# The zero shifts of a query slot as a step of their own on SyncE, in a two-layer transformer block kernel

## What is computed

```python
def layer(x, c, context):
    x = x + gate_a * attention(modulate(ln(x)), modulate(ln(x)))   # layer 0: gate from c; layer 1: rotary q and k, no gate
    x = x + attention(ln(x), context)                              # layer 0: ln(context); layer 1: rotary, modulated
    return x + gate_m * mlp(modulate(ln(x)))                       # layer 0: tanh gelu, gate; layer 1: erf gelu, no gate

def attention(q_in, kv_in):
    q, k, v = q_in @ Wq, kv_in @ Wk, kv_in @ Wv                    # 16 heads of 8
    return softmax(q @ k.T / sqrt(8)) @ v @ Wo
```

## Time and profile before

| What | us |
|---|---|
| three runs, lowest, median, highest | 380.88, 382.94, 384.89 |
| the profiled execution, whole | 385.06 |
| its span, from the first to the last instruction | 383.3 |
| TensorE busy | 363.0 |
| VectorE busy | 301.7 |
| ScalarE busy | 254.5 |
| GpSimd busy | 100.6 |

### The profile page before, as it was taken

The page is one execution under the profiler, slowest core; times in us unless marked ns, Lnnn a source line. Parts: engine busy times, 40 slices in busy tenths (PEclk is TensorE's granted clock), DMA queues, the critical chain, the costliest instruction groups (busy, mean ns, idle before and its releaser), DMA issues.

```text
span 383.3 us, 12514 instructions
## 1 busy us (share of the span) xinstructions
PE 363.0 (95%) x5090; PEld 260.6 (68%) x5090; DVE 301.7 (79%) x809; ACT 254.5 (66%) x513; POOL 100.6 (26%) x120
## 2 busy tenths in 40 slices
PE   7699999999999999999999999999999899999996
PEld 3485687677776776657654567666677577886776
DVE  5985989999999998947999839997799747875302
ACT  2525965578676987889453797378766945688551
POOL 6920310142020201125351234343413401031130
PEclk9966999999999999999999999999999957999999
DMA  8673244005221360014050140403140404000003
GB/s 208 259 240 93 78 140 167 9 27 186 84 88 43 127 219 5 3 32 169 2 193 6 29 168 7 169 5 106 65 168 4 168 8 159 8 3 3 2 0 111
DMA packets 19757, 34.13 MB, mean 89 GB/s; under 512 B 2740, under 2 KB 7988, under 8 KB 19700
## 3 DMA queue, kind: packets, MB, share of 16 engines
q1 hardware_dynamic: 19268, 33.24, 25.2%
q10 hardware_dynamic: 432, 0.09, 0.2%
HBM read 6.51 MB, written 1.05 MB: 20 GB/s over the span
## 4 chain that ended last, share of the span: by engine, by line
PE 55%; DVE 4%; ACT 3%; DMA 3%; SPq 3%; issue 2%; ACTq 0%; DVEq 0%
PE ps_ao L1058 11%; PE ps_misc L999 8%; PE ps_misc L1028 6%; PE ps_misc L1109 6%; PE ps_misc L1087 6%; PE ps_misc L1025 6%; PE ps_misc L935 3%; PE ps_misc L1094 3%; DVE maxima L690 3%; PE ps_misc L1068 2%; PE ps_misc L1007 2%; ACT PT L882 2%; DMA Ks<-Kl 2%; DMA Ks<-Kh 1%; SPq L537 1%
## 5 line engine op out<-in xcount | busy, mean ns | idle before, releaser
L690 DVE TENSOR_REDUCE maxima<-ps_misc 128x4 f32<-128x512 f32 (+1 forms) x256 | 153.5, 664 | 17.6 <-PE ps_misc L1025 17.1
L882 ACT ACTIVATE PT<-ps_misc 128x512 f32<-128x512 f32 (+1 forms) x256 | 131.7, 606 | 24.0 <-PE ps_misc L1028 22.7
L1058 PE MATMUL ps_ao<-PT,V 120*18 120x128 f32 (+1 forms) x2048 | 70.5, 282 | 0.5 <-ACT PT L882 0.5
L1025 PEld LDWEIGHTS ps_misc<-Ks,Qd 32*128 32x128 f32 x1024 | 41.9, 197 | 30.8 <-issue 11.3
L1025 PE MATMUL ps_misc<-Ks,Qd 32*128 32x128 f32 (+1 forms) x1024 | 53.4, 298 | 8.5 <-DMA Ks<-Kl 3.3
L1058 PEld LDWEIGHTS ps_ao<-PT,V 120*18 120x18 f32 (+1 forms) x2048 | 52.6, 101 | 7.4 <-issue 2.3
L1028 PEld LDWEIGHTS ps_misc<-Qd,Ks 32*128 32x128 f32 (+1 forms) x1024 | 38.0, 186 | 21.5 <-issue 13.7
L752 POOL TENSOR_SCALAR vareps<-mv 128x4 f32<-128x4 f32 (+1 forms) x28 | 6.4, 228 | 170.9 <-DVE mv L595 170.6
L1028 PE MATMUL ps_misc<-Qd,Ks 32*128 32x128 f32 (+1 forms) x1024 | 48.7, 287 | 1.5 <-DVE maxima L690 0.8
L866 ACT ACTIVATE xnT<-ps_misc,vec 128x128 f32<-128x128 f32 x80 | 30.1, 462 | 15.6 <-PE ps_misc L935 15.5
L999 PE MATMUL ps_misc<-xnT,Wr 128*128 128x512 f32 x72 | 37.5, 641 | 1.8 <-ACT xnT L866 1.6
(11 more groups left out here) (83 smaller groups left out, 449.7 us busy)
## 6 DMA issues: line engine op xcount, KB each, us to landing
Qd<-Qh SPq DMA_DIRECT2D x32, 256.0 KB
Ks<-Kh SPq DMA_DIRECT2D x16, 256.0 KB, 2.9
Qd<-Ql SPq DMA_DIRECT2D x16, 256.0 KB
Ks<-Kh SPq DMA_DIRECT2D x16, 240.0 KB, 2.4
Ks<-Kl SPq DMA_DIRECT2D x8, 256.0 KB, 3.0
Ks<-Kl SPq DMA_DIRECT2D x8, 240.0 KB, 2.5
x<-x_in SPq DMA_DIRECT2D x4, 256.0 KB, 6.0
W<-weights SPq DMA_DIRECT2D x2, 512.0 KB, 5.0
```

The lines of the kernel that those rows point to most:

```text
L690: dve.tensor_reduce(maxima[:, h, st.b % HB, c, :], bank(use + c)[:, 0:NG * ns].rearrange("p (n k) -> p n k", n=NG), AX_X, ALU.max, negate= ...
L882: act.activation(PT[0:ns, k % PSLOTS, c, :, :].rearrange("p n t -> p (n t)"), bank(use + c)[0:ns, :], ACT.Exp, scale=SCALE).then_inc(S["pr ...
L1025: ins = pe.matmul(bank(st.use + c)[:, n * ns:(n + 1) * ns], queries, keys, start=True, stop=True)
L1058: last = pe.matmul(ps_ao[32 * c:32 * c + PAIR, block * P:(block + 1) * P], heads[:, at:at + PAIR], PT[0:ns, k % PSLOTS, c, n, :], start=no ...
```

## The change

The DMA of the zeros leaves the step `qhmove.f`. A new kind of step, `zmove.f`, issues it, after a wait for the last scores of unit f - 2 (and, for unit 2, for `no_shift`). It no longer waits for the high part of q. Fourteen such steps, `zmove.2` to `zmove.15`, stand in SyncE's list. Nothing else in the list changes order; the waits of `qhmove.f` stay.

```diff
+        ... ldt.2 khmove.2 zmove.2 mmove.1.0 qlmove.2 qhmove.2 klmove.2 ld.rows mmove.1.1 zmove.3 qhmove.3 qlmove.3
+        khmove.3 klmove.3 mmove.2.0 mmove.2.1 mmove.3.0 klmove.4 zmove.4 khmove.4 ldw.attn3 qhmove.4 qlmove.4 mmove.3.1
+        mmove.4.0 zmove.5 qlmove.5 klmove.5 qhmove.5 khmove.5 mmove.4.1 zmove.6 mmove.5.0 qhmove.6 mmove.5.1 qlmove.6
+        khmove.6 klmove.6 khmove.7 zmove.7 ldw.mlp1 qhmove.7 qlmove.7 klmove.7 mmove.6.0 mmove.6.1 zmove.8 mmove.7.0
+        ldt.0 mmove.7.1 qhmove.8 qlmove.8 zmove.9 khmove.8 klmove.8 qhmove.9 ldt.1 khmove.9 klmove.9 qlmove.9 mmove.8.0
+        mmove.8.1 mmove.9.0 ldt.3 zmove.10 qhmove.10 khmove.10 qlmove.10 klmove.10 mmove.9.1 zmove.11 qhmove.11
+        khmove.11 qlmove.11 klmove.11 mmove.10.0 mmove.10.1 mmove.11.0 klmove.12 zmove.12 khmove.12 qhmove.12
+        qlmove.12 mmove.11.1 mmove.12.0 zmove.13 qhmove.13 qlmove.13 klmove.13 khmove.13 mmove.12.1 mmove.13.0
+        zmove.14 qhmove.14 klmove.14 khmove.14 qlmove.14 mmove.13.1 khmove.15 zmove.15 klmove.15 mmove.14.0
+        qlmove.15 qhmove.15 mmove.14.1 mmove.15.0 mmove.15.1 ...
...
-                        if high and st.f >= KSLOTS:
-
-                            if st.f == KSLOTS:
-                                sp.wait_ge(S["no_shift_ready"], 1)
-                            sp.dma_start(f32(Qd[SPLIT:P:TROWS, st.f % KSLOTS, :, :]),
-                                         no_shift[:, None, :].to_broadcast([HG, NG, CT])
-                                         ).then_inc(S[f"queries_in{st.f % KSLOTS}"], 16)
                         src = Qh if high else Ql
                         for part in (0, 2) if high else (1,):
                             sp.dma_start(f32(Qd[part:P:ROW, st.f % KSLOTS, :, :]),
                                          f32(src[:, st.f % 2, :])).then_inc(S[f"queries_in{st.f % KSLOTS}"], 16)
+                    elif st.kind == "zmove":
+                        sp.wait_ge(*last_score(st.f - KSLOTS))
+                        if st.f == KSLOTS:
+                            sp.wait_ge(S["no_shift_ready"], 1)
+                        sp.dma_start(f32(Qd[SPLIT:P:TROWS, st.f % KSLOTS, :, :]),
+                                     no_shift[:, None, :].to_broadcast([HG, NG, CT])
+                                     ).then_inc(S[f"queries_in{st.f % KSLOTS}"], 16)
```

More of the change, by code:

```diff
@@ L182 @@
         ldc.1 ld.x3 ld.x2 ld.bqk ld.mod1 ldw.mlp0 khmove.0 qhmove.0 klmove.0 qlmove.0 klmove.1 khmove.1 qhmove.1
[L183 to L191, removed]
@@ L192 @@
-        mmove.14.1 mmove.15.0 mmove.15.1 store.m6 store.m5 store.m4 store.m7""",
+        qlmove.1 ldc.0 ldc.3 ldc.2 mmove.0.0 ldw.attn2 ld.Wb ld.rope mmove.0.1 ldt.2 khmove.2 zmove.2 mmove.1.0
+        qlmove.2 qhmove.2 klmove.2 ld.rows mmove.1.1 zmove.3 qhmove.3 qlmove.3 khmove.3 klmove.3 mmove.2.0
+        mmove.2.1 mmove.3.0 klmove.4 zmove.4 khmove.4 ldw.attn3 qhmove.4 qlmove.4 mmove.3.1 mmove.4.0 zmove.5
+        qlmove.5 klmove.5 qhmove.5 khmove.5 mmove.4.1 zmove.6 mmove.5.0 qhmove.6 mmove.5.1 qlmove.6 khmove.6
@@ new lines @@
+        klmove.6 khmove.7 zmove.7 ldw.mlp1 qhmove.7 qlmove.7 klmove.7 mmove.6.0 mmove.6.1 zmove.8 mmove.7.0 ldt.0
+        mmove.7.1 qhmove.8 qlmove.8 zmove.9 khmove.8 klmove.8 qhmove.9 ldt.1 khmove.9 klmove.9 qlmove.9 mmove.8.0
+        mmove.8.1 mmove.9.0 ldt.3 zmove.10 qhmove.10 khmove.10 qlmove.10 klmove.10 mmove.9.1 zmove.11 qhmove.11
+        khmove.11 qlmove.11 klmove.11 mmove.10.0 mmove.10.1 mmove.11.0 klmove.12 zmove.12 khmove.12 qhmove.12
+        qlmove.12 mmove.11.1 mmove.12.0 zmove.13 qhmove.13 qlmove.13 klmove.13 khmove.13 mmove.12.1 mmove.13.0
@@ L193 @@
+        zmove.14 qhmove.14 klmove.14 khmove.14 qlmove.14 mmove.13.1 khmove.15 zmove.15 klmove.15 mmove.14.0
+        qlmove.15 qhmove.15 mmove.14.1 mmove.15.0 mmove.15.1 store.m6 store.m5 store.m4 store.m7""",
 }
```

## The result

The changed kernel takes 385.92 us (median of 20 runs, 381.82 to 389.71), the kernel before beside it 383.80 us (20 runs, 379.84 to 387.16): 2.1 us more. The means of all 20 runs are 385.59 and 383.89 us, a ratio of 1.0044. The change makes the kernel slower, by 0.4 to 1%. The forecast was 382.9 us with a range to 385.8; the time lies 0.1 us above that range. Of the 3.0 us between forecast and time, 0.9 us stood in the starting point: the kernel before has a median of 382.94 us in the three runs shown ahead of the prediction and 383.80 us in the 20. The profiled execution of after took 385.52 us, with a span of 383.7 us at a mean granted clock of 0.964.

The account below looks back on a forecast made before the run. TensorE, busy for 95% of the span, was taken to set the time, so SyncE changes pay only where it waits for moves. The terms summed to 0 (-1.0 to +0.9 us), giving 382.9 us, range 379.9 to 385.8.

Parts of the forecast that it names:

- the fourteen places: The issues of zeros in slots 2 to 15: all on the chain would be 8.4 us, but they aren't.
- The three kinds of slots: Same place: 3, 10, 11, 13, 14; issued back to back: 2, 4, 5, 7, 12; waited for something later: 6, 8, 9, 15.
- this one stage: Low clock behind max.14.0's 1.71 us of idle: 4.2 us, about the runs' spread, hit in some runs and not others.
- Slot 8: The only place where a gain could be, ahead of max.8.0: 0 us, from -0.4 to +0.6.
- The exit of the zeros from the head: Start of slot 8's burst: q high goes at 174.82, q low is issued by 177.0; 0.6 us given back.
- The zeros of slot 9 in the middle: Between q low 8 and k high 8: they take the 0.6 us that slot 8's zeros give back.
- 0.4 us of lag: Slot 8's burst: zeros at the head hold four engines for 1.0 us, 0.6 us of it ahead of the next issue.
- The rival on the slower side: Slot 8: a late score.7.3 lets the zeros of slot 9 hold the k moves; 388.0 us, chance 0.10.
- The deciding point: max.8.0: score.7.3 0.9 us later brings idle to 1.71 us, where the clock fell at slot 14; below, a small loss.
- the estimate from the same page: Slot 8: 8 KB per engine take some 0.28 us, zeros nearly free in mid-burst, a sum of -0.4 us.
- Slots 2 and 7: Back-to-back slots: zeros pass mmove.1.0 in 2, 0 us (0 to +0.2), and a weight load in 7, 0.
- The sum: All terms over the kernel: 0 us, from -1.0 to +0.9, carried to the runs' median of 382.94 us.

Follow-up runs that it names:

- rest_new: The changed kernel with the zeros of slots 8 and 9 back in qhmove.f, ahead of the high parts: 382.88 us, 1.0005 of the kernel before.
- z9_home: The changed kernel with the zeros of slot 9 moved behind k low 8, directly ahead of q high 9: 383.39 us, 0.9951 of the kernel before.
- busy8: The changed kernel with one extra, overwritten product on TensorE ahead of the wait of max.8.0: 385.40 us, 1.0079 of the kernel before.
- mid4x2: The changed kernel with a second 32 KB copy of the zeros directly behind those of slot 9 in mid-burst: 1.0174 of the kernel before.
- z9_wait_only: The changed kernel with only the wait for score.7.3 in mid-burst, the zeros of slot 9 behind k low 8: 1.0036 of the kernel before.
- before_busy14: The kernel before with one extra, overwritten product on TensorE ahead of the wait at max.14.0: 381.88 us, 0.9979 of the kernel before.
- mid16: The changed kernel with slot 9's zeros behind k low 8 and another 32 KB copy over 16 engines in mid-burst: 1.0048 of the kernel before.
- only_z9: The kernel before with only the zeros of slot 9 moved, between q low 8 and k high 8: 384.53 us, 1.0096 of the kernel before.

## Why the prediction was wrong, point by point

**What bounds the kernel, and the fourteen places: right.** The three kinds of slots hold. rest_new, with twelve moved zeros, is at 1.0005, and max.14.0, whose zeros come back to the same place, stands still for 1.59 us after 1.71. That the runs' spread is the clock, read without proof, holds: at equal clock a standard deviation of 2.7 us shrinks to 0.7. That it is this one stage, hit or not, is too narrow: the granted clock fell behind max.14.0 in 13 of 14 traces, for 3.4 to 13.7 us, and low stretches elsewhere came and went too (in z9_home's trace near 10, 34, 72 and 85 us).

**Slot 8: the step that failed.** Its sum was 0 (-0.4 to +0.6). It was put together from three terms, against the table:
1. *The exit of the zeros from the head brings q low forward by 0.6 us.* It brought 0.3 in after (2.46 against 2.76 from release to the end of q low's issue) and 0 in busy8. In the eight bursts without zeros at the head it was 2.46 to 3.03, median 2.69, mid4x2's 3.41 apart; in the three with them 2.76 to 2.82. The working had q low issued 2.2 us behind the release (177.0 - 174.82), from a pair of q high at "the 1.51 us of now" and 0.6 us for q low; with nothing ahead of it that pair took 1.98 to 2.78 us or, in after and z9_home, 1.22 with a q low of 0.85 to 0.93 behind it. In its place the traces show the load of code, whose end q high or q low followed with the zeros at the head and without: the 0.57 us of the zeros had cost next to nothing there. The prediction didn't name the load, which also runs in the stretch of the earlier trace rows that it read as the zeros alone.
2. *The zeros of slot 9 in the middle take one issue, 0.6 us.* They took 0.65. Right.
3. *At the head 0.4 us of lag, in the middle 0.33 to 1.0, so about the same.* Head 4.36 - 3.83 = 0.5, middle 4.5 - 3.8 = 0.7, so +0.14 for the change. Right in size, as far as single executions tell (z9_home's 4.40 has neither).

The term that was mis-sized is the first: 0.6 us of credit, of which 0 to 0.3 came. With it the sum is (-0.3 to 0) + 0.65 + 0.14 = +0.49 to +0.79 us; that is no test of its own but how the table adds up for after (+0.48) and busy8 (+0.78). The value for slot 8 was wrong; its upper bound of 0.6 holds in the one and not in the other. What took the time past the range of the whole is, beside the 0.9 us in the starting point, the way from slot 8 to the end (the last point below).

**The rival on the slower side: right place, wrong mechanism and wrong price point.** The zeros of slot 9 did hold the k moves of slot 8, but not by a late score.7.3: z9_wait_only shows that the wait is free. The deciding point was set at 1.71 us of idle at max.8.0, as the clock had stayed up after 0.84 and fallen after 1.71. The granted clock fell after 1.32 us in after and, at max.14.0, after 0.96 us in before_busy14. The two cases bounded the point; the upper bound was taken for the point itself.

**The Trainium skill's rule against the row.** The Trainium skill (DMA: Bandwidth & Descriptors, section Why a DMA increments its semaphore by 16 and not by 1) has an outermost size of 4 run on four engines. The share of 0.29 in after agrees. By the estimate from the same page of the Trainium skill, section Specifications, the zeros would have been nearly free in mid-burst; that rate holds for the pieces of the k moves and of mid16's copy, and not for the zeros, which ran at 8.8 GB/s an engine and cost 0.7 us. For this term the bounds from the rows (0.33 to 1.0) held.

**Slots 2 and 7: small terms.** Slot 2 was bounded by 0.2: score.1.0 now waits for the move of maxima, and is 0.18 us later than in the earlier trace rows, of which 0.07 was there in the step ahead of it:

```profile
47.48 1.14 SPq L569 DMA_DIRECT2D Qd<-maxT  x2
...
50.35 0.53 PEld L1029 LDWEIGHTS ps_misc<-Qd,Ks 32*128 32x128 f32 x16 [0.32 <-DMA Qd<-maxT]
```

In slot 7 max.7.0 came 0.26 us later in after's profile, as q low's issue took 1.59 us there; it was taken as 0. z9_home and mid16, with the same order there, have no such wait, so it isn't steady.

**The total.** The sum added slot 8's microseconds to the total one for one. The local loss is 0.5 to 0.8 us, and the kernel lost 2.1 us of median, 1.7 of mean; at equal clock it is 1.4, for only_z9 1.8 against 1.2 in its slot. That the loss grows on its way to the end is shown by only_z9, beside whose runs those of before have their clock on record; for after it rests on before's clock in later runs. That the low clock at slot 8 is part of it fits after's trace and isn't confirmed by busy8, and why the loss at equal clock is more than that of the slot stays open.

## What to carry to other kernels

Cost a DMA put into a running burst by its issue (0.65 us here, whatever its size) and by how long its pieces hold their engines (0.7 us of delay for 32 KB in four pieces to an engine, none seen for one piece to each of 16), and don't credit the place that it leaves until you have seen what the next issue waits for: here it was a load of code that no line of the kernel names. An idle TensorE wait is not a fixed price: read each wait next to the clock behind it, and treat the gap between the longest harmless and the shortest harmful one as unknown. Where runs spread by more than the effect, compare them at equal granted clock.

## What the runs showed of the hardware

- A DMA of 32 KB took SyncE as long to issue as one of 256 KB (0.60 against 0.54 us in mid16), so small moves are not small in a queue.
- In ten of twelve traces the issue of the pair of q high in slot 8 ended 0.38 to 0.41 us behind the end of a load of 16 KB of code, whatever was issued ahead of it. Behind it the engines ran empty: in only_z8, where the load ended at 172.79 and the second part of q high was issued by 173.19, the DMA share was 0.05 from 173.0 to 173.6, until the second part's bytes moved.

```profile
172.00:173.00 1.00, 1.00 (x33) 0.72 (x22) 1.00 (x4) 1.00 (x3) 0.36 (x1) 1.00 0.68 250
173.00:173.60 0.60, 0.60 (x7) 0.60 (x7) 0.21 (x1) 0.60 (x3) 0.28 (x1) 1.00 0.05 10
173.60:174.40 0.80, 0.80 (x10) 0.80 (x9) 0.00 (x0) 0.80 (x3) 0.80 (x1) 1.00 0.71 266
```

- Pieces of 2 KB took 0.085 us in the moves of k and 0.26 to 0.39 us in the zeros, from the second one on an engine; why isn't known.
- The time at low clock differs between runs of the kernel before from 1 to 34 us, and each us of it cost 0.33 us of span.
